# Fusion stage of a four-layer token mixer: products laid out as 128 + 64 features, the 64-wide rests of two samples in each half of the partitions

## The reference

```python
q = elu(x @ W_q_lin + b_q) + 1
k = elu(x @ W_k_lin + b_k) + 1
v = x @ W_v_lin + b_v
s = q @ k.T
lin = (s @ v) / (s.sum(-1) + 1e-6)
gate = sigmoid(relu(concat([lin, o, x]) @ W_g1 + b_g1) @ W_g2 + b_g2)
h = h + (o + gate * (lin - o)) @ W_out + b_out
```

## Time and profile before

| what | value |
|---|---|
| three timed runs | 1792.51 us median, 1791.17 to 1795.49 |
| profiled execution | 1795.81 us, of which the span of the core is 1793.8 us |
| PE busy in the span | 1633.9 us (91%) in 13530 instructions |
| DVE, ACT, POOL busy | 986.3 us (55%), 742.5 us (41%), 573.9 us (32%) |
| mean granted clock of TensorE | 0.95 of full |
| the fusion stage | from 882.5 us to about 1110.7 us of the span |

### The profile page before, as it was taken

How to read it: one execution, slowest core, us unless ns; L and a number is a source line. 1 busy time by engine, 2 the same in 40 slices (tenths; PEclk the granted TensorE clock), 3 DMA queues, 4 the chain that set the end, 5 groups by cost and what they waited for, 6 DMA issues and landing times. The chain is left out here.

```text
span 1793.8 us, 35834 instructions
## 1 busy us (share of the span) xinstructions
PE 1633.9 (91%) x13530; PEld 1122.5 (63%) x13530; DVE 986.3 (55%) x2733; ACT 742.5 (41%) x1420; POOL 573.9 (32%) x547
## 2 busy tenths in 40 slices
PE   7999799999996999889898787999999999889996
PEld 4677579976654899657555453222224775558886
DVE  2487722226748222368436655888886766942221
ACT  1266223324531111145424445999994553211111
POOL 1231122225412442364001113555552101325553
PEclk9999789999996999999988988999999999999998
DMA  6000455521005455112100115999992004026662
GB/s 230 1 2 2 165 172 182 181 83 30 18 2 206 172 181 179 59 27 105 48 1 19 43 51 175 401 394 360 355 331 75 2 2 156 1 74 192 191 188 33
DMA packets 97458, 228.21 MB, mean 127 GB/s; under 512 B 24297, under 2 KB 55753, under 8 KB 96393
## 3 DMA queue, kind: packets, MB, share of 16 engines
q1 hardware_dynamic: 77527, 206.13, 32.3%
q0 software_dynamic: 19552, 19.63, 4.5%
q10 hardware_dynamic: 210, 0.15, 0.0%
HBM read 198.91 MB, written 26.56 MB: 126 GB/s over the span
## 5 line engine op out<-in xcount | busy, mean ns | idle before, releaser
L2832 ACT ACTIVATE l2s_hidden<-ps,pack_l2f 128x816 f32<-128x816 f32 x256 | 226.8, 937 | 18.4 <-PE ps L2756 8.8
L2851 POOL TENSOR_TENSOR l2s_gated<-l2s_hidden,l2s_whole 128x408 f32<-128x408 f32 x128 | 136.6, 1068 | 103.4 <-PE ps L2764 103.4
L116 PE MATMUL ps<-pack_const 128*128 128x512 bf16 x574 | 146.1, 406 | 16.2 <-PEq L150 5.9
L2874 DVE TENSOR_TENSOR l2s_gated<-l2s_hidden,l2s_whole 128x816 f32<-128x816 f32 x128 | 142.1, 1110 | 28.0 <-ACT l2s_hidden L2832 25.7
L2331 POOL DMA_INDIRECT l_xt<-rows_in,l_tokens x66 | 63.1, 956 | 244.8 <-PE ps L2344 186.9
L2372 PE MATMUL ps<-l_down,l_hidden 128*128 x792 | 139.8, 327 | 0.0
L2372 PEld LDWEIGHTS ps<-l_down,l_hidden 128*128 128x128 f32 x792 | 127.3, 190 | 0.4
L116 PEld LDWEIGHTS ps<-pack_const 128*128 128x128 bf16 x574 | 56.7, 103 | 87.5 <-issue 37.5
L2355 PE MATMUL ps<-l_xtT,l_up 128*128 128x128 f32 x792 | 99.5, 276 | 3.4 <-DVE l_xtT L2607 3.4
L2355 PEld LDWEIGHTS ps<-l_xtT,l_up 128*128 128x128 f32 x792 | 96.7, 192 | 4.4 <-DVE l_xtT L2607 4.4
L2451 ACT ACTIVATE l_hidden<-ps,l_down 128x128 f32<-128x128 f32 x198 | 54.6, 374 | 90.1 <-PE ps L2360 90.0
(11 more groups left out here) (523 smaller groups left out, 3597.8 us busy)
## 6 DMA issues: line engine op xcount, KB each, us to landing
l2s_whole<-g_whole SPq DMA_DIRECT2D x128, 612.0 KB, 6.6
l_up<-in_l_up SPq DMA_DIRECT2D x66, 576.0 KB, 3.7
l3c_wg<-in_l_gate SPq DMA_DIRECT2D x16, 576.0 KB, 4.9
l3c_wu<-in_l_up SPq DMA_DIRECT2D x16, 576.0 KB, 6.4
l3c_wd<-in_l_down SPq DMA_DIRECT2D x16, 576.0 KB, 3.8
slots_out<-l_y SPq DMA_DIRECT2D x66, 96.0 KB, 2.3
l_down<-in_l_down SPq DMA_DIRECT2D x8, 675.0 KB, 8.6
l_down<-in_l_down SPq DMA_DIRECT2D x8, 576.0 KB, 7.1
```

The source lines that it names most:

```text
L116: pe.matmul(bank, halves[:, 0:128], halves[:, :], start=True, stop=True)
L2832: act.activation(hidden[:, p % kept, :, :], ps[:, 0, 2 * (p % 2):2 * (p % 2) + 2, 0:NG], ACT.Gelu_apprx_tanh, bias=w.at("b1")[:, s * MT + ...
L2851: pool.tensor_tensor(gated[:, (4 * n + 1) % ring, :], hidden[:, 2 * n % kept, 1, :], whole[:, n % ahead, 0, :], ALU.mult).then_inc(late_re ...
L2874: dve.tensor_tensor(gated[:, at:at + 2, :], hidden[:, (2 * n + 1) % kept, :, :], whole[:, n % ahead, 1:3, :], ALU.mult).then_inc(gated_rea ...
```

## The change

Every product of the stage on 96-partition tiles is laid out as the input is: 128 features ("wide") and 64 ("rest"). The wide part of a quad has 408 columns. The rests of samples 0 and 1 stand in partitions 0 to 63 and those of samples 2 and 3 in partitions 64 to 127, so that they need 204 columns. The weights are laid out to match on the host. The concatenation of `lin` and `o` becomes `MIX` = 3 blocks of 128, of which the middle one is 64 features of each. Below are the lines that the change adds, with what stays around them; what they replace stands in the functions of the same names above (`hidden_wide` and `hidden_rest` replace `hidden_part`). `gate_products` and `out_products` now both call `paired_products`, with `hidT` and `wg2`, and `fT` and `wo`.

```diff
@@ fusion_and_gates: tiles and banks @@
+lin_x = spare["l1a"].take(128, 2, NG + 2 * L)
+mixT, fT = spare["l0f"].take(128, MIX, NG), spare["l0f"].take(128, NG + 2 * L)
+hidT = spare["l0a"].take(128, NG + 2 * L)
+lin_f = m.sb("lin_f", [128, 2, NG + 2 * L])
...
+def lin_bank(side):
+    return ps[:, 1, side, 0:NG]
+def lin_rest(side):
+    return ps[:, 1, 2, 2 * side * L:2 * (side + 1) * L]
+def hid_bank():
+    return ps[:, 1, 0, 0:NG]
+def hid_rest():
+    return ps[:, 0, 1, 0:2 * L]
+def wide_of(tile, b):
+    return tile[:, b * L:(b + 1) * L]
+def rest_of(tile, b):
+    return tile[REST * (b // 2):REST * (b // 2 + 1), NG + b % 2 * L:NG + (b % 2 + 1) * L]
+def pair_half(q, a, rest=None):
+    there = slice(q * GB + 2 * a, q * GB + 2 * a + 2)
+    return xT[:, 0, there, :] if rest is None else xT[half_rows(rest), 1, there, :]
...
@@ tensor engine @@
     def lin_products(q):
+        weights = w.at("lin_wq", 2), w.at("lin_wk", 2)
+        for side, wt in enumerate(weights):
+            if q and side:
+                pe.wait_ge(lin_o_ready, q)
+            pe.matmul(lin_bank(side), wt[:, 0, 0:WIDE], turned(q), start=True, stop=False)
+        for side, wt in enumerate(weights):
+            pe.matmul(lin_bank(side), wt[half_rows(side), 1, 0:WIDE], turned(q, side), start=False, stop=True,
+                      tile_position=(REST * side, 0)).then_inc(lin_ps, 1)
+        for side, wt in enumerate(weights):
+            for a in range(2):
+                pe.matmul(lin_rest(side)[half_rows(a)], wt[:, 0, WIDE:D], pair_half(q, a), start=(side == 0), stop=False,
+                          tile_position=(0, REST * a), skip_group_check=True)
+        for side, wt in enumerate(weights):
+            for a in range(2):
+                last = pe.matmul(lin_rest(side)[half_rows(a)], wt[half_rows(0), 1, WIDE:D], pair_half(q, a, 0),
+                                 start=False, stop=True, tile_position=(0, REST * a), skip_group_check=True)
+        last.then_inc(lin_ps, 1)
...
@@ lin_values, lin_scores @@
+                    pe.wait_ge(lin_x_ready, 4 * q + 2 + 2 * side)
...
+        pe.wait_ge(v_ready, q + 1)
         if q:
             pe.wait_ge(hid_ready, 2 * (q - 1) + 1)
+        for first in range(2):
+            for side in range(2):
+                b = first + 2 * side
+                pe.matmul(ps[0:L, 1, side, first * L:(first + 1) * L], wide_of(lin_f[:, 1, :], b), wide_of(lin_f[:, 0, :], b),
+                          start=(first == 0), stop=False, skip_group_check=True)
+        for first in range(2):
+            for side in range(2):
+                b = first + 2 * side
+                last = pe.matmul(ps[0:L, 1, side, first * L:(first + 1) * L], rest_of(lin_f[:, 1, :], b),
+                                 rest_of(lin_f[:, 0, :], b), start=False, stop=True, tile_position=(REST * side, 0),
+                                 skip_group_check=True)
...
+    def hidden_wide(q, n):
+        if n < MIX:
+            return pe.matmul(hid_bank(), w.at("wg1", MIX)[:, n, 0:WIDE], mixT[:, n, :], start=False, stop=(n == MIX - 1))
+        pe.matmul(hid_bank(), w.at("wg1x", 2)[:, 0, 0:WIDE], turned(q), start=True, stop=False)
+        return pe.matmul(hid_bank(), w.at("wg1x", 2)[half_rows(0), 1, 0:WIDE], turned(q, 0), start=False, stop=False,
+                         tile_position=(0, 0))
+    def hidden_rest(q, n):
+        for a in range(2):
+            cols = slice(2 * a * L, 2 * (a + 1) * L)
+            if n < MIX:
+                last = pe.matmul(hid_rest()[half_rows(a)], w.at("wg1", MIX)[:, n, WIDE:D], mixT[:, n, cols],
+                                 start=(n == 0), stop=False, tile_position=(0, REST * a))
+            elif n == MIX:
+                last = pe.matmul(hid_rest()[half_rows(a)], w.at("wg1x", 2)[:, 0, WIDE:D], pair_half(q, a),
+                                 start=False, stop=False, tile_position=(0, REST * a))
+            else:
+                last = pe.matmul(hid_rest()[half_rows(a)], w.at("wg1x", 2)[half_rows(0), 1, WIDE:D], pair_half(q, a, 0),
+                                 start=False, stop=True, tile_position=(0, REST * a))
+        return last
     def mix_transposes(q):
         pe.wait_ge(lin_o_ready, q + 1)
         if q:
             pe.wait_ge(y_added, q)
+        for n in range(MIX):
             if n == 2:
                 if q + 1 < G:
                     pe.wait_ge(lin_x_ready, 4 * (q + 2))
+                hidden_wide(q, MIX)
+                pe.wait_ge(mixT_ready, MIX * q + 1)
             for b in range(GB):
+                into = ps[:, 0, n % 2, b * L:(b + 1) * L]
+                if n == 1:
+                    pe.matmul(into[half_rows(0)], lin_o[:, b, WIDE:D], ident[0:L, 0:L], start=True, stop=True,
+                              tile_position=(0, 0))
+                    last = pe.matmul(into[half_rows(1)], o[:, q * GB + b, 0:REST], ident[0:L, 0:L], start=True, stop=True,
+                                     tile_position=(0, REST))
+                else:
+                    src = o[:, q * GB + b, REST:D] if n else lin_o[:, b, 0:WIDE]
+                    last = pe.transpose(into, src, ident[0:L, 0:L])
             last.then_inc(mixT_ps, 1)
     def gate_hidden(q):
+        for n in range(MIX):
+            pe.wait_ge(mixT_ready, MIX * q + n + 1)
+            last = hidden_wide(q, n)
         last.then_inc(hid_ps, 1)
+        for n in range(MIX + 2):
+            last = hidden_rest(q, n)
         last.then_inc(hid_ps, 1)
+    def paired_products(src, wt):
+        for first in range(2):
+            for side in range(2):
+                b = first + 2 * side
+                pe.matmul(pair_rows(0, 0, b), wide_of(src, b), wt[:, 0, :], start=True, stop=False)
+            for side in range(2):
+                b = first + 2 * side
+                last = pe.matmul(pair_rows(0, 0, b), rest_of(src, b), wt[half_rows(side), 1, :], start=False, stop=True,
+                                 tile_position=(REST * side, 0))
+        return last
...
@@ fused_transposes @@
+        for b in range(GB):
+            last = pe.transpose(ps[:, 0, 0, b * L:(b + 1) * L], gate[:, b, 0:WIDE], ident[0:L, 0:L])
+        last.then_inc(fT_ps, 1)
+        for b in range(GB):
+            last = pe.matmul(ps[half_rows(b // 2), 0, 1, b % 2 * L:(b % 2 + 1) * L], gate[:, b, WIDE:D],
+                             ident[0:L, 0:L], start=True, stop=True, tile_position=(0, REST * (b // 2)))
+        last.then_inc(fT_ps, 1)
...
@@ scalar engine @@
+        if q:
+            act.wait_ge(lin_f_ready, q)
+        for side, name in enumerate(("lin_bq", "lin_bk")):
+            act.wait_ge(lin_ps, 3 * q + side + 1)
+            act.activation(lin_x[:, side, 0:NG], lin_bank(side), ACT.Identity, bias=w.at(name)[:, 0:1])\
+               .then_inc(lin_x_ready, 1)
+        act.wait_ge(lin_ps, 3 * q + 3)
+        for side, name in enumerate(("lin_bq", "lin_bk")):
+            act.activation(lin_x[:, side, NG:NG + 2 * L], lin_rest(side), ACT.Identity, bias=w.at(name)[:, 1:2])\
                .then_inc(lin_x_ready, 1)
...
     def mix_copies(q):
+        for n in range(MIX):
+            act.wait_ge(mixT_ps, MIX * q + n + 1)
+            act.activation(mixT[:, n, :], ps[:, 0, n % 2, 0:NG], ACT.Copy).then_inc(mixT_ready, 1)
     def hidden(q):
+        act.wait_ge(hid_ps, 2 * q + 1)
+        act.activation(hidT[:, 0:NG], hid_bank(), ACT.Relu, bias=w.at("bg1")[:, 0:1]).then_inc(hid_ready, 1)
+        act.wait_ge(hid_ps, 2 * q + 2)
+        act.activation(hidT[:, NG:NG + 2 * L], hid_rest(), ACT.Relu, bias=w.at("bg1")[:, 1:2]).then_inc(hid_ready, 1)
...
     def fused_copies(q):
+        act.wait_ge(fT_ps, 2 * q + 1)
+        act.activation(fT[:, 0:NG], ps[:, 0, 0, 0:NG], ACT.Copy).then_inc(fT_ready, 1)
+        act.wait_ge(fT_ps, 2 * q + 2)
+        act.activation(fT[:, NG:NG + 2 * L], ps[:, 0, 1, 0:2 * L], ACT.Copy).then_inc(fT_ready, 1)
...```

VectorE's `lows` and `features` are not edited, but their tiles `lin_x` and `lin_f` have 1224 columns on 128 partitions now, not 1632 on 96.

The first place is TensorE's program for `lin_products` and `lin_values` of one quad. The names are the two tiles of a product, `xT_all` the transposed input and `pack_l2a` the weights, then the partitions and columns of the result, then how many such products follow each other. Before:

```order
L1623 MATMUL ps<-xT_all,pack_l2a 96x408 x2
L1626 MATMUL ps<-xT_all,pack_l2a 96x408 x2
L1623 MATMUL ps<-xT_all,pack_l2a 96x408 x2
L1626 MATMUL ps<-xT_all,pack_l2a 96x408 x2
L1635 MATMUL ps<-pack_l2a,xT_all 102x192 x2
L1639 MATMUL ps<-pack_l2a,xT_all 102x192 x2
```

More of the change, by code:

```diff
@@ L1675, in mix_transposes @@
                     pe.wait_ge(y_added, q)
-                for n in range(2 * C):
+                for n in range(MIX):
                     if n == 2:
@@ L1700, in gate_products @@
             def gate_products(q):
                 pe.wait_ge(hid_ready, 2 * (q + 1))
-                for b in range(GB):
-                    for c in range(C):
```

(24 more changed lines are left out.)

76 lines of the change are left out of this document (11 added, 65 removed).

## The result

| | before | changed |
|---|---|---|
| median of nine timed runs | 1796.19 us (1791.17 to 1806.56) | 1783.56 us (1775.67 to 1786.31) |
| ratio, 95% interval | | 0.9917 (0.9893 to 0.9942) |
| profiled span | 1793.8 us | 1782.1 us |

The changed kernel is faster by 0.83%, with 0.58% to 1.07% as the interval. The nine runs of the kernel before have a median 3.7 us above the three shown ahead of the prediction, so the ratio is the fairer comparison: 1792.51 x 0.9917 is 1777.6, against the forecast 1777.3.

What follows compares the result with a forecast made beforehand. TensorE (PE) was taken to set the pace in the fusion stage. Savings of 2.1 + 11.1 + 1.7 + 0.4 = 15.3 us gave 1777.3 us for the timed median (1792.51 - 15.2), range 1772 to 1785.

Steps and rivals of the forecast that it cites:

- Term 1: `lin_products` and `lin_values`: 0.7 us saved in each of quads 1, 2 and 3, 2.1 us in all.
- The unknown price: Whether two column tiles on the same 64 rows (L1651, L1716) overlap; overlap taken, none would cost 4.1 us in all.
- rival 1: The 64-row column pairs do not overlap: 11.2 us gained, 1781 us; chance 0.15.
- rival 2: No column pair overlaps, because loads and products wait for each other: 1792 us; chance 0.04.
- Term 2: Transposes and hidden product: 2.84 us saved beside quads 1 and 2, 3.0 beside quad 3, 2.4 last; 11.1 together.
- Term 3: Quad 0: scores start 1.1 us earlier and take 2.5 us instead of 3.09; together 1.7 us saved.
- Term 4: End of a quad, `paired_products`, `out_products` and fused transposes with their copies: net gain of 0.4 us.
- Rival 3: Saved time is absorbed by late `features` and a longer rest-copy stall: 6.6 us lost, 1784 us; chance 0.08.
- Rivals 4 and 5: 4: more work at low clock, slower, chance 0.06; 5: low stretch goes or router chain profits, 1771 us, chance 0.05.

Runs made afterwards that it cites:

- halves_in_turn: Changed kernel with `gate_hidden`'s column-tiled products reordered, all ten left-half passes, then ten right, instead of in turn; ratio 0.9964 to the kernel before.
- more_fill: Changed kernel with 22 instead of 10 filling products ahead of the last router steps; ratio 0.9868 to the kernel before, median 1774.61 us.

## Why the prediction was right, and where its parts were not

**Direction and size.** The forecast was a gain of 15.2 us; 0.83% of 1792.51 is 14.9. The stage became 16.1 us shorter against 15.3. The mechanism held: fewer passes, and column halves that overlap. That the sum came so close is in part luck. Stretches that left the low clock beside quads 1 and 3 gave 4.6 us that were not forecast, and the low clock in the last quad took 4.2 back.

**Term 1** was 2.1 us and is 2.2, with luck: 0.7 of it is low clock that only the old quad 2 had (8.56 us against 7.87 in quad 3). At full clock it is 0.5 a quad, not 0.7. The products take 4.13 instead of 4.04, and the stall for ScalarE, which is 0.35 and replaces 0.18, ends at 5.05 us from the start and not at 4.84. **The unknown price**: the pair of column halves on the same 64 rows overlaps (0.84), so rival 1 falls, and with it rival 2. The rule of the Trainium skill, TensorE: Matmul & The Clock Gate, under "What overlaps and what doesn't", would have given 1792; the runs speak for the other one, in the Trainium skill, TensorEngine Tiling, under "Key Properties". `halves_in_turn` adds a condition: five products on one side and then five on the other did not overlap, where alternating ones did.

**Term 2** was 11.1 us and is 10.4, from parts that were off both ways. At full clock the group takes 7.67 and not 7.35. The price of a pass was right: inside L1700 beside quad 2 the passes start at 944.52, 944.87, 945.21 and 945.55 us, 0.34 apart, as in the old layout. What was too small is the changes of form between the groups. The two passes of L1701 take 0.88 us where I took 0.78, L1700 takes 2.17 for six where I took 2.06, because its last pass takes 0.44, and the two groups of four transposes take 0.45 and 0.41 and not 0.35 each. Less the 0.1 that I had added for one more change, that is 0.3 us a quad. In quad 2 the 1.7 us at the low clock, which I said "stay", went. In the last quad "2.4" was 0.35, for the clock: `more_fill` shows it.

**Term 3** was 1.7 and is 1.58, again with luck. The changed kernel's stage began at the low clock (L1641 takes 2.26 at the start of quad 0 against 1.56 in quad 3), so the scores start 10.62 us into it, only 0.25 earlier than before and not 1.1. But the scores, start to end of both lines, take 1.76 us, almost all at full clock, instead of 3.09 where I had 2.5. In `more_fill`, whose stage begins at full clock, the two are as forecast: the scores start at 9.90 us and take 2.65.

**Term 4** was a gain of 0.4 us and is one of about 1.9 with all that was not foreseen: `out_products` beside quad 1 fell from the low clock to the full one (5.45 busy to 2.66), and in the last quad the stretch behind the hidden product became 2.2 us longer, most of it in `out_products`, now mostly at the low clock (4.21 us, 1051.51 to 1055.72, where the old one took 2.61). One step of it was wrong in its mechanism: I wrote that the identity products of `fused_transposes` "fill one half and then the other, so hardly overlap: 0.35 + 0.70". They overlap fully:

```profile
927.79 0.57 PE L1775 MATMUL ps<-pack_const,rows_z 102*128 102x102 f32 x4 [1.28 <-DVE rows_z L2078]
928.28 0.58 PE L1778 MATMUL ps<-pack_const,rows_z 102*64 102x102 f32 x8
```

Eight passes in 0.58 us, about as in the earlier trace rows where they alternate (0.57). Four passes of 102 columns on one side do not keep the four on the other out; ten of 204 do.

**Rival 3** (absorbed) did not happen: the wait for `features` stands in quad 0 alone, 2.46 us instead of 2.88. **Rivals 4 and 5** both happened in part: stretches left the low clock (beside quads 1 and 3) and others fell into it (the last quad). Together the clock in the stage stayed at 0.86, inside the 0.84 to 0.88 forecast, which hides that it moved. The stage up to the last `out_products` took 169.4 us, forecast 169.

## What to carry to other kernels

Of half-width products that stand in the two column halves of the array, those of one half are nearly free if they alternate with those of the other in the program. In a row of ten passes on one side and then ten on the other each cost its full price here. When work in front of a fixed wait is made shorter, look at the clock behind the wait first: here the layout and the filling of that wait are worth 16 and 8.5 us of the stage, and a reordering showed 5.0 us with the waits filled and 1.7 without. Price passes and changes of form apart: a pass from the middle of a long row (0.34 us in both layouts here), and every change between groups by itself, since a layout of more and shorter groups has more of them.

## What the runs showed that was not expected

- Parts of a change do not add up in a stage with two clock levels: 17.2 and 7.2 us apart, 16.1 together, in part because the same low stretches go with either part.
- How long a row on one column half may be and still let the other half's passes run beside it lies between four passes of 102 columns (0.58 us for both halves) and ten of 204 in three groups (4.03 us, no overlap).
- A change of form costs 0.17 us between pairs of row halves and full products (2.66 to 2.31 for two changes less).
- The attention ahead of the stage, which no edit touched, took 130.1 to 136.7 us from its first transpose in 14 profiles, at clocks of 0.92 to 0.97: a spread of two fifths of the effect measured here. What decides it before the kernel reaches them stays open.
